# Filler products, a moved reduction, a moved root and a swapped pair at the start of a gated cross-attention kernel

## What is computed

```python
x = x + tanh(g_xattn[0]) * xattn(layernorm(x), ctx, ctx, mask, Wq, Wk, Wv, Wo, bo)
x = x + tanh(g_ffn[0])  * ffn(layernorm(x), Wg, bg, W1, b1, W2, b2)

# xattn: qh, kh, vh = heads of q@Wq, k@Wk, v@Wv
dots = einsum('bhid,bhjd->bhij', qh, kh) * d**-0.5
dots = where(mask, -max, dots);  out = (softmax(dots) @ vh) @ Wo + bo
# ffn: one expert of eight for each token
idx = argmax(softmax(xf @ Wg + bg)); h = gelu(xf @ W1 + b1); y = h @ W2 + b2; out = y[idx]
```

## Time and profile before

| | us |
|---|---|
| median of 3 runs | 218.99 |
| lowest and highest | 217.61, 219.11 |
| the profiled execution's own time | 218.79 |
| its span in the profile | 217.0 |
| TensorE busy | 192.1 (89%) |
| VectorE busy | 124.2 (57%) |
| ScalarE busy | 103.8 (48%) |
| GpSimd busy | 89.4 (41%) |

### The profile page before, as it was taken

One profiled execution on the slowest core, in us unless ns is written; L12 is line 12 of the kernel. 1 busy time (PEld: TensorE's weight loads), 2 busy tenths in 40 slices (PEclk: granted clock), 3 DMA queues, 4 the chain that ended last, 5 costly groups with the idle time before them and its releaser, 6 DMA issues.

```text
span 217.0 us, 3916 instructions
## 1 busy us (share of the span) xinstructions
PE 192.1 (89%) x1236; PEld 138.0 (64%) x1236; DVE 124.2 (57%) x525; ACT 103.8 (48%) x372; POOL 89.4 (41%) x129
## 2 busy tenths in 40 slices
PE   0089999979999999999999889999999999979950
PEld 0044349465677554488896456766688999959940
DVE  0578922578998642234327889899935337255520
ACT  0211333679999811401134799899561244435510
POOL 7000090157667790000000599765950001777560
PEclk9999999999999999999999999999999999999996
DMA  4993184999999600083000011600000000254111
GB/s 114 349 394 138 32 251 169 287 318 307 327 254 252 226 2 0 3 273 114 0 0 5 0 49 52 187 14 2 0 3 2 0 0 0 101 167 141 35 52 21
DMA packets 21185, 25.16 MB, mean 116 GB/s; under 512 B 1875, under 2 KB 19741, under 8 KB 21024
## 3 DMA queue, kind: packets, MB, share of 16 engines
q1 hardware_dynamic: 19136, 22.51, 34.0%
q0 software_dynamic: 1152, 2.12, 2.9%
q10 hardware_dynamic: 864, 0.15, 0.4%
HBM read 14.14 MB, written 11.68 MB: 119 GB/s over the span
## 4 chain that ended last, share of the span: by engine, by line
PE 64%; ACT 16%; DVE 10%; DMA 3%; issue 3%; POOL 1%; POOLq 0%; DVEq 0%
ACT probs L768 13%; PE o_bank L1526 13%; PE s_bank L1567 12%; PE s_bank L1866 6%; PE o_bank L1877 6%; PE o_bank L1648 4%; PE s_bank L1674 4%; DVE probs L1225 3%; PE s_bank L1607 3%; PE t_bank L1623 3%; DMA rows<-in_x_dram 3%; PE o_bank L1641 2%; PE s_bank L1855 2%; PE t_bank L1656 2%; PE t_bank L1544 1%
## 5 line engine op out<-in xcount | busy, mean ns | idle before, releaser
L608 POOL TENSOR_TENSOR probs<-probs,r_col 128x512 f32<-128x512 f32 x32 | 33.3, 1042 | 66.4 <-DVE r_col L1236 65.2
L768 ACT ACTIVATE probs<-probs,negm_run 128x160 f32<-128x160 f32 x128 | 53.0, 415 | 6.9 <-DVE negm_run L1225 6.9
L1225 DVE CUSTOM_DVE_ANT_0 probs<-s_bank,maskneg 128x160 f32<-128x160 f32 x128 | 32.6, 320 | 2.3 <-PE s_bank L1607 2.3
L1567 PE MATMUL s_bank<-xnT,wq_sb 128*128 128x512 f32 x64 | 31.6, 645 | 1.3 <-ACT q_sb L728 0.7
L1526 PE MATMUL o_bank<-wo_sb,oT 128*128 128x256 f32 x128 | 28.6, 379 | 0.0
L1526 PEld LDWEIGHTS o_bank<-wo_sb,oT 128*128 128x128 f32 x128 | 23.9, 190 | 3.5 <-issue 0.5
L768 ACT ACTIVATION_READ_ACCUMULATOR probs<-probs,negm_run 128x1 f32 x128 | 23.9, 187 | 0.0
L1567 PEld LDWEIGHTS s_bank<-xnT,wq_sb 128*128 128x128 f32 x64 | 12.8, 207 | 17.0 <-issue 15.5
L1607 PE MATMUL s_bank<-k_sb,q_sb 64*128 64x160 f32 x256 | 22.0, 311 | 0.0
L1607 PEld LDWEIGHTS s_bank<-k_sb,q_sb 64*128 64x128 f32 x256 | 17.9, 186 | 4.6 <-issue 4.0
L1623 PE MATMUL t_bank<-ident,probs 128*128 128x128 f32 x128 | 17.9, 281 | 1.8 <-issue 1.1
(11 more groups left out here) (148 smaller groups left out, 287.8 us busy)
## 6 DMA issues: line engine op xcount, KB each, us to landing
sorted_rows<-empty_row SPq DMA_DIRECT2D x8, 1040.0 KB, 14.0
oT<-in_L_ffn_W_dram SPq DMA_DIRECT2D x1, 2048.0 KB, 18.5
q_sb<-in_L_ffn_W_dram SPq DMA_DIRECT2D x1, 2048.0 KB, 8.5
oT<-sorted_rows SPq DMA_DIRECT2D x1, 1040.0 KB, 6.5
oT<-sorted_rows SPq DMA_DIRECT2D x8, 130.0 KB, 2.1
rows<-in_x_dram SPq DMA_DIRECT2D x2, 512.0 KB, 9.2
wq_sb<-in_L_xattn_Wq_dram SPq DMA_DIRECT2D x1, 1024.0 KB, 9.0
mask_sb<-in_mask_BxSxS_bk_dram SPq DMA_DIRECT2D x2, 512.0 KB, 11.6
```

The source lines that it names most:

```text
L608: nc.gpsimd.tensor_tensor(window_wide(u), window_wide(u), r.rearrange("p i h -> p (i h)") .unsqueeze(2).broadcast_to([P, 4, WIDE]), ALU.mult)
L768: last = nc.scalar.activation(window_part(u, i, h), window_part(u, i, h), ACT.Exp, bias=negm_run[at], scale=-1.0, accum_out=l_run[at])
L1225: nc.vector.tensor_tensor_reduce(window_part(u, i, h), s_bank[u % 2][:, h, i * CK:i * CK + WK], maskneg[:, q, 0:WK], -SCALE, LARGEST, ALU. ...
L1567: last = nc.tensor.matmul(bank[m % 4], wq_sb[:, c, m * P:(m + 1) * P], xnT[:, c, b * N:(b + 1) * N], start=(c == 0), stop=(c == DC - 1))
```

## The change

Five edits:

- TensorE waits first for the eps and the ones only (`ident_ready` at 2), and runs 22 products of ones by ones, 128x128, into `bank[0]`, ahead of its old wait. Two more follow `xn_transposes(0)`. Nobody reads the results; the first projection overwrites the bank.
- `visit_sums()` moves from behind m = 2 into m = 4, between its two products. The transposes of b1 move from behind m = 2 to behind m = 4.
- VectorE copies q tile 3 before `find_windows()` instead of behind the statistics of batch 1.
- ScalarE does the second root and the tanh behind its third q copy (m = 4) instead of its first.
- TensorE transposes batch 1 of x ahead of the context of batch 0.

```diff
             for m in range(0, M, 2):
                 take_q(0, m)
-                if m == 0:
+                if m == 4:
                     std1(1)
                     act.wait_ge(s_small, 16 * 5)
                     nc.scalar.activation(gate[:], gate_in[:], ACT.Tanh).then_inc(gate_ready, 1)
...
             take_q(0, 1)
+            take_q(0, 3)
             find_windows()
             dve.wait_ge(b1_ps, 1)
...
             variance(range(QT, TT))
-            take_q(0, 3)
             norm(QT, TT, xn, ln_ready)
...
+            def keep_busy(count):
+
+                for _ in range(count):
+                    nc.tensor.matmul(bank[0][:, 0:P], ones[:], ones[:], start=True, stop=True)
+
+
+            pe.wait_ge(ident_ready, 2)
+            keep_busy(22)
             pe.wait_ge(ident_ready, E + 3)
...
             xn_transposes(0)
+            keep_busy(2)
             pe.wait_ge(s_wq, 16)
             pe.wait_ge(pro_act, 1)
...
                 for c in range(DC):
+                    if b == 0 and m == 4 and c == 1:
+                        visit_sums()
                     if b == 0 and m == 0 and c == 1:
...
             for m in range(M):
                 project_q(0, m)
-                if m == 2:
-                    visit_sums()
+                if m == 4:
                     pe.wait_ge(s_b1, 16)
...
             def rest(later_too):
 
+                xn_transposes(1)
                 if later_too:
                     context(first, 0, 0)
                 else:
                     window_context(0)
-                xn_transposes(1)
```

## The result

| | before | changed |
|---|---|---|
| median of 10 executions | 218.97 us | 216.23 us |
| lowest, highest | 217.61, 219.23 | 214.72, 217.89 |
| profiled execution, span | 218.79, 217.0 | 214.72, 213.0 |

The ratio to the kernel before is 0.9898 (95% interval 0.9862 to 0.9933): 1.0% faster, where 1.8% was forecast. The median of 216.23 us lies inside the range given (214.2 to 216.6); the gain is little more than half of the forecast one. In three more comparisons of the same two kernels the ratio was 0.9845 (0.9803 to 0.9888), 0.9866 (0.9842 to 0.989) and 0.9901 (0.987 to 0.9931). So the change is faster each time, by 1.0 to 1.6%, and its own times spread over 3 us. Three executions that stand far above the others of their kernel (221.09 us in e3, 255.29 in e8, 393.32 of the kernel before, beside e5 to e8) are left out of the ratios, but not out of the medians.

The account below looks back on a forecast made before the run. Bound by a chain of waits, x's load and normalisation, then TensorE, partly at half rate. Keys earlier by 0.5 + 2.9 + 0.85 + 0.2 - 0.7 = 3.8 us; 218.79 - 3.8 = 215.0 us, range 214.2 to 216.6.

Parts of the forecast that it names:

- part 1: Products of ones before x's transposes: raise the clock early, saving 0.5 us at the transposes and 2.9 us in the projection.
- Does the clock survive the pause: Between the products' end and TensorE's old start at 10.38, up to 1.4 us: clock taken as kept, having outlived 3.8 us.
- The sign of the products' own clock: Clock rise between 6.7 and 9.3 us, so the 22 products end at 9.0 to 10.3, before 10.38, and cost nothing.
- Products hidden, transposes faster, half rate gone: Start to projection: two extra products hidden in a 0.82 us wait, transposes save 0.5 us, projection at full rate saves 2.9.
- Projection to its end: Query projection of batch 0: starts at 12.4, ends m = 7 at 26.6, where it was 31.08.
- Block sums: Inside m = 4: TensorE arrives at 20.15, minima ready at 19.9, cover 0.2 us; window search at 21.1, 0.3 us earlier.
- The second root: ScalarE's root and tanh moved behind its third q copy: TensorE's stall before m = 6 goes, 0.85 us.
- Context and second batch: Before the keys: batch 1's transposes go first, ScalarE's context copy no longer hidden, about 0.7 us idle, keys at 29.05.
- Rival 1: No clock won: late rise or a fall in the pause, projection starts at half rate; 218.7 us, no change; chance 0.10.
- Rival 3: Given back later: a stage after the keys is tied to something unmoving; end gains perhaps 2 us, 216.8; chance 0.08.
- Theory D: Theory tried in the follow-up runs: the keys' gain is lost further down the kernel, in every execution.

Follow-up runs that it names:

- e3: Kernel before with the 22 and 2 products of ones added and none of the moves: 217.46 us, ratio 0.9975 to the kernel before.
- e8: Changed kernel with the context's transposes ahead of batch 1's again: median 216.44 us, ratio 0.9875 to the kernel before.
- e5: Changed kernel with 12 products of ones instead of 22: 217.18 us, ratio 0.9915 to the kernel before.
- e6: Changed kernel run again without edit, six executions: 215.98 us; its traced execution had a late x and a full clock.
- e12: Changed kernel run again without edit, one traced execution, in which the clock fell: 217.32 us, mean clock 0.978.
- e7: Changed kernel with the second root and tanh back behind ScalarE's first q copy: 221.68 us, ratio 1.0127 to the kernel before.
- e2: Changed kernel without any products of ones or the wait for the ones, all moves kept: 217.61 us, ratio 0.9978 to the kernel before.
- e10: Changed kernel with products spread over the pause, q tile 3 copied behind second statistics, context ahead of batch 1: 215.03 us, ratio 0.9834 to the kernel before.
- e9: Changed kernel with the products spread over the pause by waits for x and its variances, second run: 216.01 us, ratio 0.9864 to the kernel before.

## Why the prediction was right and wrong

The direction and the main mechanism were right, and the size was not: the ratio of the first comparison is a gain of 1.0%, with an interval up to 1.4%, against 1.8%. The step that failed is "so I take it as kept" in part 1: in about one execution of four the clock fell in the pause. A second term was mis-sized, the projection's duration, by 0.45 us in every execution. Means add up, so they show the shares: in the first ten executions of each kernel the mean went from 218.73 to 216.49, a gain of 2.24 us, 1.56 short of 3.8. Without the four executions with a low clock the mean is 216.01, so the falls make 0.48 of it, the projection makes 0.45, and about 0.6 stays open. Part of it is one slow execution at 0.985 (217.61), and part may lie behind the output projection. Even without a fall the forecast was 0.8 us too high: the two profiled executions with a late x and no fall went from 218.79 to 215.79 (e6), 3.0 us.

- **Does the clock survive the pause: wrong, and the step that failed.** It read 3.8 us of survival off the end of the kernel and concluded for a shorter pause: "The pause is shorter, so I take it as kept." e12 shows a fall with a pause of 2.29 us before the transposes, 3.5 us after the last product; e5 shows it 2.9 us after the last product. One observation at the end of a kernel is not a lower bound, and the ends of the other traces show how far it was from one. In e3 TensorE's last group ends at 206.86, and the windows read:

```profile
207.00:209.00 2.00, 0.00 (x0) 0.00 (x0) 0.46 (x1) 0.00 (x0) 1.43 (x2) 0.97 0.32 75
209.00:211.00 2.00, 0.00 (x0) 0.00 (x0) 0.00 (x0) 0.00 (x0) 0.54 (x1) 0.50 0.27 61
```

A mean of 0.97 over 207 to 209 is a fall at 208.9, 2.0 us after the last work. Worked out in the same way, the 14 traces give 2.0 to 4.4 us; the trace before, with 3.9, was one of the longest. The price of a fall is 1.2 us at the keys (23.32 against 22.08 us).
- **The sign of the products' own clock.** An early rise is bad luck: the products then run out sooner and the pause is longer. The prediction computed both ends (9.0 and 10.3), but held the early end for the harmless one. In four of the eight traces with 22 products they ended at 7.7 to 8.5 (8.0 in e12), before its range, so a rise carried over from one trace (6.7 to 9.3) came out too late. The trace before does have transposes alone, eight from 10.38, but at the lower rate; that the prediction missed them changes nothing.
- **Products hidden, transposes faster, half rate gone: right.** Projection at 12.50 in e6 (12.4 forecast), extra products hidden behind ScalarE's copy.
- **Projection to its end, 14.2 us forecast (26.6 - 12.4): 14.6 in e6.** Eighteen passes take 7.9 us instead of 7.74, the two behind the block sums 1.06 instead of 0.86, and the last twelve 5.26 (21.87 to 27.13) instead of 5.16. So each group that starts behind a wait or a small product loses 0.1 to 0.2 us; the prediction had seen that once (3.53 for eight passes) and put it under rounding. This is the 0.45 us by which the keys are late with a full clock (22.08 against 29.05 - 7.41 = 21.64 from the statistics).
- **Block sums: right.** Reached at 20.40 in e6 (20.15 forecast), no wait. VectorE's last row for the minima starts at 20.05 there, so the cover stayed as thin as forecast. The window search started at 21.35 and not at 21.1, which is 0.06 us and not 0.3 ahead of before; it cost nothing here, since x's transposes now come ahead of the context's.
- **The second root: right as a sum, wrongly priced as a part.** 0.85 us was the old stall. With TensorE early, the old place of the root costs 3.6 us of stall and 1.4 of clock (e7). Without this move the changed kernel would have been slower than before. Each part was priced as if the others stood as before; in e2 and e3 neither half comes to 0.3% by the ratio, nor to more than 0.7% by the interval.
- **Context and second batch: right times, wrong merit.** Keys 2.42 us after m = 7 in e6 (2.45 forecast), with the 0.7 us of idle time foreseen. But the forecast didn't put the old order beside it: it is equal (e8), and with the search 0.4 us sooner the keys come 0.7 us earlier (e10).
- **Rival 1** happened, in part of the executions and at less than its price: the clock fell when the projection was about to begin and came back at 14.9, so 1.2 us were lost and not 3.8. A chance for a kernel is the wrong form for something that varies from execution to execution; a quarter of the executions at 1.2 us each belonged into the sum as 0.3 us.
- **Rival 3** (Theory D): refuted up to the output projection, where 0.07 us of the shift is lost. Behind it the changed kernel's traces take 0.2 to 0.8 us longer than the only one of before. All other kernels' traces lie above that one too (e5 the nearest, 184.35 from keys to end against 184.18), so it may just be a short one; one trace of before can't settle it.

## What to carry to other kernels

Filler products that keep the clock up have to cover the pause by what releases it, a wait for the data and then a few more, and not by a fixed number, because the number's duration depends on the clock it is meant to raise. When TensorE is made to arrive earlier, price every wait behind it anew from the time of its producer: on the way to the keys the moves here bring 0.5 us without the products, the products 0.7 without the moves, and both 3.3. Of something that varies from execution to execution, here the clock's fall, look at every place of the trace and at several traces before a bound is read from it. And before two profiles are compared, take out the landing of the first load.

## What the runs showed of the hardware

- The load of x, the first that SP issues, released its statistics either at 5.6 to 6.0 us or at 7.3 to 7.5. Traces with the same code fell on either side (the changed kernel three times early, twice late); it shifts the whole execution by 1.5 us. What decides it is open.
- The clock fell 2.9 us (e5) and 3.5 us (e12) after the last product, near the end of a 3.63 us stall (e7), and at the ends of the kernels 2.0 to 4.4 us after TensorE's last work. It held over gaps of up to 0.78 us (e9), 0.94 (e3) and 1.22 (e6). In e12 eight transposes ran at full rate from 10.31 and did not keep it from falling at 11.5. The Trainium skill ("TensorE: Matmul & The Clock Gate", Part 4: PE-mode transpose) says that transposes don't count as TensorE activity as products do. This trace agrees with it but doesn't prove it, as the fall came 3.5 us after the last product, within the 2.0 to 4.4 us seen with no work at all, and no run put products in the transposes' place.
- VectorE's scaling of the mask (128x640, uint8 to bf16) took 0.49 us in the kernel before and 3.4 to 4.1 us in every trace where GpSimd's 4.5 us addition to x ran beside it (3.85 in the changed kernel's timeline above), and it ended about 0.35 us after the addition each time. In e7 the stall put it behind that addition, and it took 0.49 again, as it did in e3; VectorE's row in e7:

```profile
32.70 0.49 DVE L1257 TENSOR_SCALAR maskneg<-mask_sb 128x640 bf16 x1 [1.12 <-issue]
```

No experiment moved the addition alone, so that the two collide is read from these traces and not isolated. It cost nothing that shows: the output projection of the second batch comes 126.53 us after the keys with it (e6) and 126.52 without (e7).
